# The second LayerNorm's normalisation moved from VectorE to ScalarE, and the gate broadcast of the FFN spread over three PSUM banks

## The reference

```python
def _layernorm(x): return (x - mean(x)) / sqrt(var(x) + 1e-5)

x = x + attn(_layernorm(x))               # q, k, v = x Wq^T, x Wk^T, x Wv^T; causal softmax(q k^T / 32) v

y = _layernorm(x)
logits = einsum('bsd,ed->bse', y / norm(y), c_norm) + einsum('bsd,ed->bse', y, w_route)
gates  = softmax over the 2 largest of the 8 logits, 0 elsewhere
h      = gelu(einsum('bsd,edh->bseh', y, w1) + b1)           # 8 experts x 512 hidden units
out    = einsum('bse,bsed->bsd', gates, einsum('bseh,ehd->bsed', h, w2) + b2)
x = x + out
```

## Time and profile before

| what | us |
|---|---|
| median of 2 runs | 2384.87 (2383.7 to 2386.04) |
| the profiled execution, its own time | 2386.06 |
| span of its slowest core, from the first to the last instruction | 2384.5 |
| spans of its 8 cores | 2372.4 to 2384.5 |

### The profile page before, as it was taken

How to read it: one execution, slowest core, us unless ns; L and a number is a source line. 1 busy time by engine, 2 the same in 40 slices (tenths; PEclk the granted TensorE clock), 3 DMA queues, 4 the chain that set the end, 5 groups by cost and what they waited for, 6 DMA issues and landing times.

```text
span 2384.5 us, 32900 instructions; the slowest of 8 cores (2372.4 to 2384.5 us)
## 1 busy us (share of the span) xinstructions
PE 1940.4 (81%) x12448; PEld 1141.0 (48%) x12448; DVE 629.6 (26%) x1686; ACT 542.0 (23%) x1204; POOL 86.2 (4%) x129
## 2 busy tenths in 40 slices
PE   3887888945676888898935599999999999999998
PEld 2665666612233434343414255555555555555554
DVE  2322222144335233241331022222122222222221
ACT  2334333311120211212102022222111222222111
POOL 0000000000000000000010000000000000000000
PEclk9999999977888989999967799999999999999999
DMA  8212111022122121121169411111111011111100
GB/s 156 68 58 63 57 54 54 27 106 93 59 84 93 36 84 63 45 72 36 45 141 165 79 45 36 45 45 45 45 45 35 19 45 36 45 45 45 45 18 19
DMA packets 41164, 142.81 MB, mean 60 GB/s; under 512 B 4114, under 2 KB 4114, under 8 KB 37938
## 3 DMA queue, kind: packets, MB, share of 16 engines
q0 software_dynamic: 25552, 73.42, 12.6%
q1 hardware_dynamic: 15458, 67.28, 9.0%
HBM read 113.44 MB, written 50.33 MB: 69 GB/s over the span
## 4 chain that ended last, share of the span: by engine, by line
PE 68%; DVE 14%; DMA 7%; issue 5%; ACT 3%; another core or an unknown queue 2%; POOL 1%; DVEq 1%; ACTq 0%; SPq 0%; POOLq 0%
PE ph L828 20%; PE psc L538 10%; PE pout L874 9%; PE pout L876 9%; PE pqk L358 9%; PE pctx L588 3%; PE pctx L590 3%; DMA x_scr<-x2b 3%; DMA arena<-w1s 2%; DVE x2b L610 2%; DMA wqkv<-wkT 2%; DVE stt L248 1%; DVE scr L249 1%; DVE gbc L811 1%
## 5 line engine op out<-in xcount | busy, mean ns | idle before, releaser
L828 PE MATMUL ph<-ln2Tg,arena 128*128 128x256 bf16 x4096 | 492.1, 286 | 33.3 <-DMA arena<-w1s 33.3
L828 PEld LDWEIGHTS ph<-ln2Tg,arena 128*128 128x128 bf16 x4096 | 388.0, 102 | 139.7 <-issue 40.6
L846 ACT ACTIVATE hT<-ph,b_s 128x256 bf16<-128x256 f32 x512 | 243.9, 476 | 879.8 <-PE ph L828 879.8
L874 PE MATMUL pout<-arena,hT 128*128 128x512 bf16 x1024 | 389.2, 380 | 57.5 <-DMA b_s<-b 39.2
L876 PE MATMUL pout<-arena,hT 128*128 128x512 bf16 x1024 | 389.1, 380 | 0.0
L538 PE MATMUL psc<-qbuf,arena 128*128 128x512 bf16 x1152 | 275.4, 404 | 68.1 <-ACT probsT L551 60.2
L358 PE MATMUL pqk<-xlnT,wqkv 128*128 128x256 bf16 x2048 | 258.3, 292 | 68.4 <-ACT qstage L376 59.2
L588 PE MATMUL pctx<-arena,probsT 128*128 128x512 bf16 x528 | 210.2, 398 | 74.8 <-DVE x2b L610 74.8
L358 PEld LDWEIGHTS pqk<-xlnT,wqkv 128*128 128x128 bf16 x2048 | 213.1, 105 | 114.4 <-issue 73.4
L855 DVE TENSOR_TENSOR hT<-hT,gbc 128x256 bf16<-128x256 bf16 x512 | 149.8, 293 | 377.0 <-ACT hT L846 377.0
L538 PEld LDWEIGHTS psc<-qbuf,arena 128*128 128x128 bf16 x1152 | 117.2, 103 | 223.0 <-issue 115.0
(11 more groups left out here) (88 smaller groups left out, 986.8 us busy)
## 6 DMA issues: line engine op xcount, KB each, us to landing
xbuf<-x SPq DMA_DIRECT2D x32, 512.0 KB, 3.6
xr<-x SPq DMA_DIRECT2D x32, 512.0 KB, 3.6
x_scr<-x2b POOLq DMA_DIRECT2D x32, 512.0 KB, 3.8
x2g<-x_scr SPq DMA_DIRECT2D x16, 1024.0 KB, 9.7
out<-outsb POOLq DMA_DIRECT2D x32, 512.0 KB, 2.9
qt_scr<-qstage POOLq DMA_DIRECT2D x16, 512.0 KB, 3.8
qbuf<-qt_scr SPq DMA_DIRECT2D x8, 1024.0 KB, 6.1
ln2t_scr<-ln2Ts POOLq DMA_DIRECT2D x32, 256.0 KB, 3.2
```

Of the source, the lines that this page charges most:

```text
L828: mm = pe.matmul(ph[hc % 2][:, 0:256], arena[:, kd * 4096 + hc * 128: kd * 4096 + hc * 128 + 128], ln2Tg[:, gc % 2, kd, :], start=(kd == 0 ...
L846: s.activation(hT[:, hc, :], ph[hc % 2][:, 0:256], AF.Gelu, bias=b1s[:, hc:hc + 1]))
L874: pe.matmul(pout[tl][:, 0:512], lhs, arena[:, b:b + 512], start=(hc == 0), stop=False)
```

## The change

Two edits, one for each of stages 2 and 3.

In the attention, `ln2` is made by ScalarE with the form of instruction that stage 1 has in line 284, in front of ScalarE's two instructions for 1/norm. It waits for line 640 (VectorE) and for the transposes of the tile before the last (TensorE). VectorE goes from line 640 straight to line 650. The transposes now wait for ScalarE's count, and VectorE's line 606 waits, besides what it waited for, for `ln2` of tile t - 2.

In the FFN, transposing the gates and copying them to `gT2` become a function, emit_c_gates, which is called once ahead of the groups and then at the end of each group for the next one; `gT2` gets two buffers, and the copy waits for the second group back to have read its own. The four pairs of the broadcast go to the banks `pbc`, `ph[0]`, `ph[1]`, `pbc`. Pair 3 waits for the copy of pair 0; pairs 1 and 2 wait for the last gelus of the group before, which read those banks. Block 0 of the hidden units waits for the copy of pair 1 and block 1 for that of pair 2.

```diff
--- before.py
+++ after.py
@@ -422,7 +422,7 @@
 
             def emit_a2_tailA(t):
                 def a2_pe_tr(pe, t=t):
-                    pe.wait_ge(sVe.h, ln2_done[t])
+                    pe.wait_ge(sAc.h, ln2_done[t])
                     if t >= 1:
                         pe.wait_ge(sVe.h, ln2T_cp[t - 1])
                     for kd in range(KD):
@@ -601,6 +601,7 @@
                         v.wait_ge(sXr[t % 2].h, xr_ld[t])
                         if t >= 2:
                             v.wait_ge(sSl[t % 2].h, x2_store[t - 2])
+                            v.wait_ge(sAc.h, ln2_done[t - 2])
                         if t >= 1:
                             v.wait_ge(sAc.h, V["rstd2_%d" % (t - 1)])
                         w = sVe.inc(v.reciprocal(stt[:, 15:16], pctx[:, 1024:1025]))
@@ -636,17 +637,9 @@
 
                     def a2_ve2_t(v, t=t):
                         v.wait_ge(sAc.h, V["rstd2_%d" % t])
-                        w = sVe.inc(
+                        V["negmr2_%d" % t] = sVe.inc(
                             v.tensor_scalar(stt[:, 6:7], stt[:, 2:3], -1.0,
                                             stt[:, 5:6], ALU.mult, ALU.mult))
-                        V["negmr2_%d" % t] = w
-                        v.wait_ge(sVe.h, w)
-                        if t >= 2:
-                            v.wait_ge(sPe.h, ln2T_tr[t - 2])
-                        ln2_done[t] = sVe.inc(
-                            v.tensor_scalar(ln2[:, t % 2, :], x2b[:, t % 2, :],
-                                            stt[:, 5:6], stt[:, 6:7],
-                                            ALU.mult, ALU.add))
                         w = sVe.inc(v.tensor_scalar(stt[:, 8:9], stt[:, 3:4], -EPS,
                                                     stt[:, 5:6], ALU.add, ALU.mult))
                         v.wait_ge(sVe.h, w)
@@ -660,6 +653,13 @@
                     blk.vector(a2_ve2_t)
 
                     def a2_ac2_t(s, t=t):
+                        s.wait_ge(sVe.h, V["negmr2_%d" % t])
+                        if t >= 2:
+                            s.wait_ge(sPe.h, ln2T_tr[t - 2])
+                        ln2_done[t] = sAc.inc(
+                            s.activation(ln2[:, t % 2, :], x2b[:, t % 2, :],
+                                         AF.Identity,
+                                         bias=stt[:, 6:7], scale=stt[:, 5:6]))
                         s.wait_ge(sVe.h, V["t4_%d" % t])
                         w = sAc.inc(s.activation(stt[:, 10:11], stt[:, 9:10], AF.Ln))
                         s.wait_ge(sAc.h, w)
@@ -721,7 +721,7 @@
 
         with ExitStack() as pc:
             Ec = pc.enter_context
-            gT2 = Ec(nc.sbuf_tensor("gT2", [NEXP, 256], BF16))
+            gT2 = Ec(nc.sbuf_tensor("gT2", [NEXP, 2, 256], BF16))
             gbc = Ec(nc.sbuf_tensor("gbc", [128, 8, 256], BF16))
             ln2Tg = Ec(nc.sbuf_tensor("ln2Tg", [128, 2, KD, 256], BF16))
             x2g = Ec(nc.sbuf_tensor("x2g", [128, 2, 2048], F32))
@@ -759,6 +759,29 @@
             w2_done = [None] * NT
             out_ev = [None] * NT
             out_st = [None] * NT
+
+            def emit_c_gates(g):
+                def c_pe_gT(pe, g=g):
+                    pe.wait_ge(sVe.h, gates_done[2 * g + 1])
+                    if g >= 1:
+                        pe.wait_ge(sVe.h, V["gT2cp_%d" % (g - 1)])
+                    for tl in range(2):
+                        mm = pe.transpose(ptG[0:8, tl * 128:tl * 128 + 128],
+                                          gates_tm[:, (2 * g + tl) * 8:
+                                                   (2 * g + tl + 1) * 8],
+                                          ident[:])
+                    V["gTtr_%d" % g] = sPe.inc(mm)
+                blk.tensor(c_pe_gT)
+
+                def c_ve_gT(v, g=g):
+                    v.wait_ge(sPe.h, V["gTtr_%d" % g])
+                    if g >= 2:
+                        v.wait_ge(sPe.h, w2_done[2 * (g - 2) + 1])
+                    V["gT2cp_%d" % g] = sVe.inc(
+                        v.tensor_copy(gT2[:, g % 2, :], ptG[0:8, 0:256]))
+                blk.vector(c_ve_gT)
+
+            emit_c_gates(0)
 
             for gc in range(16):
                 def c_sync_g(sync, gc=gc):
@@ -774,34 +797,23 @@
                         out=x2g[:, gc % 2, :], in_=x2_scr[gc]), 16)
                 blk.sync(c_sync_g)
 
-                for tl in range(2):
-                    def c_pe_gT(pe, gc=gc, tl=tl):
-                        t = 2 * gc + tl
-                        pe.wait_ge(sVe.h, gates_done[t])
-                        if tl == 0 and gc >= 1:
-                            pe.wait_ge(sVe.h, V["gm_last_%d" % (gc - 1)])
-                        mm = pe.transpose(ptG[0:8, tl * 128:tl * 128 + 128],
-                                          gates_tm[:, t * 8:(t + 1) * 8], ident[:])
-                        V["gTtr_%d_%d" % (gc, tl)] = sPe.inc(mm)
-                    blk.tensor(c_pe_gT)
-
-                def c_ve_gT(v, gc=gc):
-                    v.wait_ge(sPe.h, V["gTtr_%d_1" % gc])
-                    V["gT2_%d" % gc] = sVe.inc(
-                        v.tensor_copy(gT2[:], ptG[0:8, 0:256]))
-                blk.vector(c_ve_gT)
-
+                gbanks = [pbc, ph[0], ph[1], pbc]
                 for pair in range(4):
                     def c_pe_gbc(pe, gc=gc, pair=pair):
                         if pair == 0:
-                            pe.wait_ge(sVe.h, V["gT2_%d" % gc])
-                        else:
-                            pe.wait_ge(sVe.h, V["gbc_cp_%d_%d" % (gc, pair - 1)])
+                            pe.wait_ge(sVe.h, V["gT2cp_%d" % gc])
+                        if pair == 3:
+                            pe.wait_ge(sVe.h, V["gbc_cp_%d_0" % gc])
+                        if gc >= 1:
+                            if pair == 1:
+                                pe.wait_ge(sAc.h, V["gelu_%d_%d" % (gc - 1, 30)])
+                            elif pair == 2:
+                                pe.wait_ge(sAc.h, V["gelu_%d_%d" % (gc - 1, 31)])
                         for e2 in range(2):
                             e = pair * 2 + e2
-                            mm = pe.matmul(pbc[:, e2 * 256:(e2 + 1) * 256],
+                            mm = pe.matmul(gbanks[pair][:, e2 * 256:(e2 + 1) * 256],
                                            sel[0:8, e * 128:(e + 1) * 128],
-                                           gT2[0:8, :],
+                                           gT2[0:8, gc % 2, :],
                                            start=True, stop=True)
                         V["gbc_mm_%d_%d" % (gc, pair)] = sPe.inc(mm)
                     blk.tensor(c_pe_gbc)
@@ -811,13 +823,16 @@
                         V["gbc_cp_%d_%d" % (gc, pair)] = sVe.inc(v.tensor_copy(
                             gbc[:, pair * 2:(pair + 1) * 2, :].rearrange(
                                 "p e c -> p (e c)"),
-                            pbc[:]))
+                            gbanks[pair][:, 0:512]))
                     blk.vector(c_ve_gbc)
 
                 for hc in range(32):
                     def c_pe_h(pe, gc=gc, hc=hc):
                         if hc == 0:
                             pe.wait_ge(sG[gc % 2].h, x2g_ld[gc])
+                            pe.wait_ge(sVe.h, V["gbc_cp_%d_1" % gc])
+                        if hc == 1:
+                            pe.wait_ge(sVe.h, V["gbc_cp_%d_2" % gc])
                         if gc == 0:
                             pe.wait_ge(sW1p[hc // 8].h, V["w1_%d" % (hc // 8)])
                         if hc >= 2:
...
@@ -901,6 +916,9 @@
                             out=out_h[t * 128:(t + 1) * 128, :],
                             in_=outsb[:, tl, :]), 16)
                     blk.gpsimd(c_gp_out)
+
+                if gc + 1 < 16:
+                    emit_c_gates(gc + 1)
 
             def fin_sync(sync):
                 sync.wait_ge(sF[0].h, sF[0].n)
```

More of the change, by code:

```diff
@@ L879, in c_pe_w2 @@
                         pe.matmul(pout[tl][:, 0:512],
-                                  gT2[0:8, tl * 128:tl * 128 + 128],
+                                  gT2[0:8, gc % 2, tl * 128:tl * 128 + 128],
                                   b2s[0:8, 0:512], start=False, stop=True)
                         mm = pe.matmul(pout[tl][:, 512:1024],
-                                       gT2[0:8, tl * 128:tl * 128 + 128],
+                                       gT2[0:8, gc % 2, tl * 128:tl * 128 + 128],
                                        b2s[0:8, 512:1024], start=False, stop=True)
```

## The result

The changed kernel took 2339.61 us (median of 11 runs, 2332.0 to 2518.25). The kernel before, run beside it, took 2400.42 (10 runs, 2383.69 to 2524.61). Part of the runs of both kernels were disturbed by a lower granted clock on some cores; undisturbed runs alone give a ratio of 0.976, with a 95% interval of 0.972 to 0.980. So the change makes the kernel faster, by 2.4% (2.0 to 2.8). That is clear of no change, but the interval ends at the 2% that the prediction takes for the least difference to be told, so a gain above that mark is only likely, not shown. The profiled executions, on which the sum was made, stand at 2386.06 and 2333.04 us: 53 us less, where 65 were predicted. The median is 19 us above the predicted 2321, outside the forecast's own range (2306 to 2336) and at the very top of the wide one (2284 to 2340).

A forecast was written before the change was run, and what follows sets the result against it. It took TensorE, with 68% of the chain, and its waits to bound the kernel. 2386.06 less 23 (attention edit) and 42 (FFN edit), clock 0, gave 2321 us; own range 2306 to 2336, wide range 2284 to 2340.

The forecast's parts named there:

- the forecast's own range: Whole run: 2306 to 2336 us around the forecast 2321, which was given a chance of 0.62.
- the wide one: Whole run: the range 2284 to 2340 us, holding the forecast and the case of the high clock surviving transitions.
- 2.8 us per transition from pair 0's chain: FFN transitions: pairs and copies overlap, so pair 0 to hidden units shortens from 4.87 us; 15 transitions give 42 us.
- I take the same cost as now, 0: FFN hidden units: low clock after transitions costs as before; bounds 35 us gained to 10 us lost.
- rival 1: FFN transitions: the high clock survives them, giving 2286 us, or in between if only in some; chance 0.20.
- 25 x 0.91 = 23 us: Attention: 16 store-closed loops, 7 group starts and two more places each shorten by 0.91 us; bounds 0 to 25 us.
- All behind it comes as much earlier: 441, the store, the next 606: Attention loop: the 0.91 us taken from VectorE passes on in full through the store to the next loop.
- the sign that the prediction gave: Attention: a loop falling from 13.96 to about 13.05 us means right; one still near 13.9 means wrong.
- rival 2: Attention: the edit gives nothing, as the store's landing or ScalarE's arm sets the loop; 2344 us, chance 0.10.
- The added wait on line 606: Attention, VectorE: waiting for work of one loop earlier and more, claimed to cost nothing.
- The hiding on ScalarE: Attention: ScalarE's added 1.24 us fits beside VectorE's arm; otherwise 7 starts pay at most 1.24 us each, 9 in all.
- Rival 4: Dense FFN stretches: granted clock sinks to 0.83, costing 175 us and giving 2496 us; chance 0.04.

The follow-up runs named there:

- e1: Changed kernel with the attention edit undone, so the FFN edit alone; ratio 0.981 (0.972 to 0.991) to the kernel before.
- e2: Kernel before with the attention edit alone; ratio 0.991 (0.982 to 1.000) to the kernel before.
- e3: Changed kernel with matmuls that nobody reads in the idle stretches of each FFN transition; ratio 0.961 (0.955 to 0.968) to the kernel before.
- e4: Changed kernel with the load of the next group's queries issued later, to run during the scores; ratio 0.966 (0.954 to 0.977) to the kernel before.
- e5: Changed kernel with the gates' transposes, copy and pairs moved into the group before's matmuls on pout; no ratio, profiled execution 2285.6 us.

## Why the prediction was off, and where it was right

**The FFN edit: right.** It said 2.8 us per transition from pair 0's chain, and nothing for the call moved up in the code. What is not hidden units fell by 2.8 us a group; the 1.9 us ahead of pair 0 stayed; from pair 0 to the hidden units 2.02 us were measured, 2.00 to 2.21 forecast. 15 transitions: 42 us for 42.

**The clock: the step "I take the same cost as now, 0" was mis-sized.** The level fell as at every transition before (rival 1 didn't come), but the blocks cost 30.70 us for 30.36, 5 us over 15 groups, which lies within the bounds given (35 gained to 10 lost). What was overlooked is that where the low stretch lies can change with the period. Before, on core 7, the clock came back to 1.00 at 2.8, 4.9 and 5.8 us into the hidden units, by turns; after, at 5.2 to 5.6 us in 12 of the 15 groups, and there it costs 2.7 us, near the worst of the three cases of the earlier trace rows. The blocks settle in this way in e1 and take turns in e2, so it goes with the FFN edit; why it settles there is not shown. e3 shows that the pause is the cause of the low clock.

**The attention edit: the step "25 x 0.91 = 23 us" failed; 15.6 us came** (14.6 in the table and 1.0 at the last tile). The price was right: first loops 0.97 us each, starts 0.99 (6.9 / 7). What failed is "All behind it comes as much earlier: 441, the store, the next 606", and with it the count. It treated 16 loops as one kind, from the row of a single loop, and passed over what the earlier trace rows says itself, that the loop ends on a landing. In the second loops the queries' load shares the landing. The store, issued 4.2 us behind the load before and 3.2 after, took 0.8 us longer to land and gained nothing: -0.3 us where 5.5 were summed. By the sign that the prediction gave,'s own loop, at 13.83 us, is a case of rival 2. That mechanism I had given to all loops or none; e2 and e4 show it for the second ones.

In the third loops 2.4 of 5.5 us came. By group, over 8 cores: in groups 1, 3 and 5 the loop fell by 0.8 to 0.9 us, as forecast. In group 4 it fell by 0.5; its store is issued late, before as after (10.28 and 9.71 us behind line 606 or 607). In group 6 seven of the eight cores now wait for pctx, so TensorE's matmuls set the pace there, and the prediction should have left that loop out as it did the last two groups. In group 2 the store landed after 4.4 to 5.8 us on every core, where it was 3.7 to 3.8. The queries aren't it (e4, 4.5 to 5.2 us). In that flight, and on every core, one packet of a queue of the kind "instruction" starts 2.1 to 3.1 us behind the store's issue. The other six traces with the edit and two buffers show the same packet on every core (2.1 to 3.9 us) and 4.4 to 6.4 us. No run moved that packet, so this is a coincidence and not a shown cause.

The added wait on line 606 was said to cost nothing. It costs 0.07 us in every loop (below), some 2 us in all. In the last two groups that is 0.4 of the 0.8 us lost; the rest sits in one loop, the third of group 7 (14.94 to 15.37 us; 15.36 to 15.38 in the median of each trace with the attention edit), and is not explained.

**The hiding on ScalarE: right.** At the group's starts, the arm with the added instruction stood level with VectorE's: 7 of 7 starts kept their gain, six with 9.0 us from x2b to the scores and one with 9.36, after 10.0 and 10.36 (the chain now goes through line 660 there in six of them).

**The sum.** 42 + 23 = 65 predicted; 42 - 5 + 16 = 53, as the profiled executions show. That it comes out to the microsecond is luck: the 3 us gained between the attention's end and the second FFN group, beyond the last tile and one transition (6.4 less 1.0 less 2.5), are about made up by +1.8 ahead of the first x2b, and neither was in the sum. Both are of the size by which executions differ: in the changed kernel's three traces the first of these stretches is 163.2, 166.2 and 163.9 us (medians over 8 cores). Rival 4 didn't come: PEclk 1.00 in the dense stretches, even in e5, where 97% of the FFN is matmul. The Trainium skill's rule in "TensorE: Matmul & The Clock Gate", section "Seeing it yourself", that three dense cores of a die bring the clock to 13/16, thus doesn't hold for the FFN stretches of these traces, with eight cores at it.

## What to carry to other kernels

A loop that closes on a DMA's landing has as many kinds as there are transfers that may lie beside it: list all its instances before multiplying one, and if a buffer is to be had, break the loop rather than shorten the engine's part of it (here 45 us in the loops against 8, though the group starts beside it took 12 us more). Where a TensorE pause lets the clock fall, the clock's cost is a term of its own that a shorter pause need not lower; remove the pause, by putting its work between matmuls that are going on, or fill it. And writing work earlier in the code does nothing while the same instruction stands ahead of it in its engine's queue.

## What the runs showed of the hardware that I had not expected

A wait that is long over is not quite free. Line 607 waits for one count more than line 606 did, five for four, and the chain shows these waits as steps of VectorE's queue about 0.07 us apart. In the loops that TensorE bounds, it starts 0.38 us after the last matmul on pctx, where it was 0.32 before; in those that a store closes, 0.23 us after the landing, where it was 0.16. Before:

```profile
1187.79 0.17 PE L593 MATMUL pctx<-arena,probsT 128*128 128x1 bf16 x1
...
1188.28 0.17 DVE L606 RECIPROCAL stt<-pctx 128x1 f32<-128x1 f32 x1 [5.16 <-PE pctx L593]
```

After:

```profile
1175.44 0.17 PE L593 MATMUL pctx<-arena,probsT 128*128 128x1 bf16 x1
...
1175.99 0.17 DVE L607 RECIPROCAL stt<-pctx 128x1 f32<-128x1 f32 x1 [6.09 <-PE pctx L593]
```

And TensorE work can cost less than none: e3's 22 added matmuls a group, some 2.4 us of work at the high clock, shortened the group by 2.5 us.
